# Layer 2: centring of the token norm and the residual sum moved from VectorE to TensorE and ScalarE

## The reference, cut to what matters

```
x   = x + L1(_gn(x))                       # _gn: group norm, 32 groups
tok = [tokens 3136, channels 192]
x1  = _layernorm(tok, g1, b1); x2 = _layernorm(tok, g2, b2)
        # mu = mean over channels; var = mean((x - mu)^2); (x - mu) * rsqrt(var + 1e-5) * g + b
x   = x1 @ W_in_x.T ; z = x2 @ W_in_z.T    # 192 -> 384
y_f = branch(x), y_b = branch(x reversed) reversed
        # branch: conv over 4 tokens, silu, 384 -> 12+16+16, softplus step size,
        # scan h = h * exp(dt * A) + dt * x * B over 3136 tokens and 16 states, y = sum(h * C) + x * D
out = ((y_f + y_b) * silu(z)) @ W_out.T + b_out
```

## Time and profile before

| | |
|---|---|
| median of 3 runs | 20129.69 us |
| profiled execution | 20123.45 us |
| its span, first to last instruction | 20121.7 us |
| mean granted TensorE clock | 0.938 |
| busy: TensorE, VectorE, GpSimd, ScalarE | 87%, 86%, 84%, 70% |
| scans (L1032) | 5376 of 2066 ns |
| outputs (L1240) | 5376 of 1769 ns |

### The profile page before, as it was taken

One profiled execution on the slowest core, in us unless ns is written; L12 is line 12 of the kernel. 1 busy time (PEld: TensorE's weight loads), 2 busy tenths in 40 slices (PEclk: granted clock), 3 DMA queues, 4 the chain that ended last, 5 costly groups with the idle time before them and its releaser, 6 DMA issues. The chain is left out here.

```text
span 20121.7 us, 179901 instructions
## 1 busy us (share of the span) xinstructions
PE 17468.9 (87%) x43392; PEld 7664.0 (38%) x43392; DVE 17219.6 (86%) x13583; ACT 13992.6 (70%) x35077; POOL 16825.7 (84%) x10932
## 2 busy tenths in 40 slices
PE   7888988889888898888988889888898888988889
PEld 3433434334343343433434334343343433434334
DVE  7988979889798897988979789797897978979789
ACT  6767767577676776767767577675776767767677
POOL 6978969789697896978969799696996979969699
PEclk9989989899899998989989899898998989989899
DMA  2313323133231332313323133231332313323233
GB/s 85 135 65 129 137 76 134 65 129 137 76 134 66 128 137 76 134 65 128 137 77 133 66 128 136 77 133 65 129 136 76 134 65 135 130 77 135 73 132 124
DMA packets 528855, 2178.88 MB, mean 108 GB/s; under 512 B 96328, under 2 KB 243424, under 8 KB 527648
## 3 DMA queue, kind: packets, MB, share of 16 engines
q1 hardware_dynamic: 527648, 2165.99, 29.8%
HBM read 1905.47 MB, written 245.63 MB: 107 GB/s over the span
## 5 line engine op out<-in xcount | busy, mean ns | idle before, releaser
L1032 DVE TENSOR_TENSOR_SCAN arena<-ps,arena 128x897 f32<-128x897 f32 x5376 | 10963.7, 2066 | 993.9 <-ACT arena L1188 761.6
L1240 POOL TENSOR_TENSOR arena<-arena 128x896 f32<-128x896 f32 x5376 | 9427.4, 1769 | 901.5 <-PE ps L962 619.8
L962 PE MATMUL ps<-arena,ident 128*128 128x448 f32 x21504 | 8979.4, 556 | 879.6 <-POOL arena L1240 876.2
L1172 ACT ACTIVATE ps<-arena,A 128x448 f32<-128x448 f32 x10752 | 6412.1, 632 | 1749.0 <-DVE arena L1032 1705.3
L962 PEld LDWEIGHTS ps<-arena,ident 128*128 128x128 f32 x21504 | 4049.3, 193 | 5473.3 <-issue 3690.3
L1232 POOL TENSOR_TENSOR arena<-arena 128x896 f32<-128x896 f32 x2688 | 4773.6, 1776 | 0.2 <-DMA arena<-bc_rows 0.2
L1021 DVE TENSOR_TENSOR arena<-ps,arena 128x896 f32<-128x896 f32 x2688 | 2868.0, 1067 | 30.4 <-ACT ps L1134 30.4
L919 PE MATMUL ps<-arena,diag 128*128 128x448 f32 x5376 | 2178.4, 549 | 154.0 <-issue 141.8
L919 PEld LDWEIGHTS ps<-arena,diag 128*128 128x128 f32 x5376 | 1014.8, 192 | 1233.9 <-issue 1097.4
L1094 ACT ACTIVATE arena<-ps,vece 128x448 f32<-128x448 f32 x672 | 423.3, 630 | 948.5 <-PE ps L919 948.5
L1188 ACT ACTIVATE arena<-arena 128x2 f32<-128x2 f32 x5376 | 1045.8, 195 | 50.9 <-DVE arena L1032 50.9
(11 more groups left out here) (160 smaller groups left out, 19406.9 us busy)
## 6 DMA issues: line engine op xcount, KB each, us to landing
arena<-bc_rows SPq DMA_DIRECT2D x1792, 896.0 KB, 5.4
x_projected<-arena SPq DMA_DIRECT2D x112, 672.0 KB, 3.5
y_forward<-arena SPq DMA_DIRECT2D x112, 672.0 KB, 3.9
arena<-x_projected SPq DMA_DIRECT2D x112, 672.0 KB, 7.7
arena<-y_forward SPq DMA_DIRECT2D x112, 672.0 KB, 4.1
x<-in_x SPq DMA_DIRECT2D x119, 336.0 KB, 3.6
x_normed<-arena SPq DMA_DIRECT2D x112, 336.0 KB, 2.8
arena<-x_normed SPq DMA_DIRECT2D x112, 336.0 KB, 4.2
```

The source lines that it names most:

```text
L962: m = e.matmul(y, ident[:, :], pr[:, q % NPR, a * T:a * T + T], start=False, stop=p == NP - 1 and a == 1)
L1032: e.tensor_tensor_scan(rev(hh[:, q % NH, 0:W2], s), rev(decays(q)[:, 0:W2], s), rev(bb[:, q % NB, 0:W2], s), car[:, k, n:n + 1] if i % NC ...
L1172: e.activation(two(decays(q))[:, a, :], dt[:, r % NDT, :], ACT.Exp, scale=Am[s][:, k, 2 * p + a:2 * p + a + 1]).then_inc(c_ex, 1)
L1240: e.tensor_tensor(pr[:, q % NPR, :].rearrange("p (a b) -> p a b", a=2), two(hh[:, q % NH, :]), cr[:, 2 * p:2 * p + 2, :], ALU.mult).then_i ...
```

## The change

The mean and its subtraction become one product with a centring matrix: `cent` holds I - 1/192 (192 x 192). `n1` is now two jobs, one for each half of 96 channels, of 4 matmul instructions each. `nc` is gone. `nq` is two steps on ScalarE at t + 1.5 (it was one at t + 1.9); each squares its half from PSUM into `tmp` and copies the half from PSUM to `nrm`; both wait for the second `n1`. In `o`, each half gets one more matmul (two instructions) that adds `x1` with the identity, and `ou` is a copy with bias on ScalarE, 0.9 slots later, instead of VectorE's sum; the store `out` is 0.9 later. In the forward half `td` has a due time 0.5 later (3.4 for 2.9 after its matmul), and `du` 0.3 later in both. The limit between banks 0 to 3 and WBANK moves from t = 0 to t = -10, so that chunk 1's `n1` (due at -0.2) takes a bank of WBANK. Two memsets of VectorE at the start of the layer's block are moved ahead of the group norm's statistics.

```diff
-        dve.append((t + 2.9, "td", i, e))
-        pool.append((t + 3.9, "du", i, e))
+        dve.append((t + (2.9 if CHUNK[i][0] else 3.4), "td", i, e))
+        pool.append((t + 4.2, "du", i, e))
...
-            dve += [(t + 1.0, "nc", i, 0)]
-            pe += [(t - 0.2, "n1", i, 0), (t + 2.1, "n2", i, 0)]
-            act += [(t + 1.9, "nq", i, 0), (t + 3.0, "nr", i, 0), (t + 4.6, "xh", i, 0)]
+            pe += [(t - 0.2, "n1", i, 0), (t - 0.2, "n1", i, 1), (t + 2.1, "n2", i, 0)]
+            act += [(t + 1.5, "nq", i, 0), (t + 1.5, "nq", i, 1), (t + 3.0, "nr", i, 0), (t + 4.6, "xh", i, 0)]
...
-                dve.append((o + 1.5, "ou", i, k))
-            sp.append((o + 2.5, "out", i, 0))
+                act.append((o + 2.4, "ou", i, k))
+            sp.append((o + 3.4, "out", i, 0))
...
-        banks = WBANK if t >= 0 else [*WBANK, 0, 1, 2, 3]
+        banks = WBANK if t >= -10 else [*WBANK, 0, 1, 2, 3]
...
-                        m = e.matmul(o[0:CP, :], ones[0:CP, 0:CP], nrm[:, i % 2, j * T:j * T + T], start=j == 0, stop=j == 1)
+                        m = e.matmul(o[0:CP, :], cent[:, j, k * CP:(k + 1) * CP], nrm[:, i % 2, j * T:j * T + T],
+                                     start=j == 0, stop=j == 1)
...
-                        m = e.matmul(o[0:CP, :], wout[:, j, k * CP:(k + 1) * CP], gy[:, j, :],
-                                     start=j == 0, stop=j == EJ - 1)
-                    m.then_inc(c_wt, 1)
+                        e.matmul(o[0:CP, :], wout[:, j, k * CP:(k + 1) * CP], gy[:, j, :], start=j == 0, stop=False)
+                    e.matmul(o[0:CP, :], ident[0:CP, 0:CP], x1[:, k, ch(c)], start=False, stop=True).then_inc(c_wt, 1)
...
-                if name == "nc":
-                    filled(w, "n1", i)
-                    b = bank_of("n1", i)
-                    o = nrm[:, i % 2, 0:T]
-                    e.tensor_tensor(o, o, ps[0:CP, b, 0:T], ALU.subtract).then_inc(c_nc, 1)
-                    o = nrm[:, i % 2, T:2 * T]
-                    e.tensor_tensor(o, o, ps[0:CP, b, 0:T], ALU.subtract).then_inc(c_wf[b], 1)
...
-                if name == "ou":
-                    filled(w, "o", i, k)
-                    b = bank_of("o", i, k)
-                    x = x1[:, k, ch(c)]
-                    e.scalar_tensor_tensor(x, ps[0:CP, b, 0:T], bout[:, k:k + 1], x, ALU.add,
-                                           ALU.add).then_inc(c_wf[b], 1)
...
                 if name == "nq":
-                    freed(w, "n1", i)
-                    w.wait_ge(c_nc, i + 1)
+                    filled(w, "n1", i, 1)
                     w.wait_ge(c_nm, 2 * i)
-                    for j in range(CJ):
-                        e.activation(tmp[:, j, :], nrm[:, i % 2, j * T:j * T + T], ACT.Square).then_inc(c_nq, 1)
+                    b = bank_of("n1", i, k)
+                    o = ps[0:CP, b, 0:T]
+                    e.activation(tmp[:, k, :], o, ACT.Square).then_inc(c_nq, 1)
+                    e.activation(nrm[:, i % 2, k * T:k * T + T], o, ACT.Copy).then_inc(c_wf[b], 1)
+                if name == "ou":
+                    filled(w, "o", i, k)
+                    b = bank_of("o", i, k)
+                    e.activation(x1[:, k, ch(c)], ps[0:CP, b, 0:T], ACT.Identity,
+                                 bias=bout[:, k:k + 1]).then_inc(c_wf[b], 1)
```

More of the change, by code:

```diff
@@ L142, in side_schedule @@
         used[b] = used.get(b, 0) + 1
-        if t < 0:
+        if t < -10:
             first = dict(used)
@@ L181, in build @@
     half = sb("half", [128, 1])
+    cent = sb("cent", [CP, CJ, C])
     wx = sb("wx", [CP, CJ, 384])
@@ L218, in build @@
         (ident, d["c_ident"]), (grp, d["c_grp"]), (ones, d["c_ones"]),
+        (cent, d["c_cent"]),
         (w0[:, :, 0:C], d["wk"]), (w0[:, :, C:2 * C], d["wv"]), (w0[:, :, 2 * C:3 * C], d["wr"]),
@@ L827, in build @@
     c_wf = [sem(f"c_free{b}") for b in range(8)]
-    c_ns, c_nc, c_nq, c_nr, c_nm = (sem("c_" + k) for k in ("nsc", "ncen", "nsq", "nrs", "nrm"))
+    c_ns, c_nq, c_nr, c_nm = (sem("c_" + k) for k in ("nsc", "nsq", "nrs", "nrm"))
     c_pad, c_xh, c_c1, c_c2, c_c3, c_c4 = (sem("c_" + k) for k in ("pad", "halo", "crel", "cexp", "cln", "csig"))
@@ L835, in build @@
     s_bl, s_cl = ([sem(f"{k}{G}") for G in range(4)] for k in ("b_loaded", "c_loaded"))
-    sems1 = [n1.v, n1.t, n1.a, c_ex, c_rs, c_bv, c_bp, c_sc, c_ca, c_mc, c_sm, c_ya, c_yv, c_wt, *c_wf, c_ns, c_nc,
+    sems1 = [n1.v, n1.t, n1.a, c_ex, c_rs, c_bv, c_bp, c_sc, c_ca, c_mc, c_sm, c_ya, c_yv, c_wt, *c_wf, c_ns,
              c_nq, c_nr, c_nm, c_pad, c_xh, c_c1, c_c2, c_c3, c_c4, c_t1, c_t2, c_t3, c_du,
@@ L969, in layer1_vector @@
         w = Waits(e)
+        for b in DECAY:
+            e.memset(ps[:, b, T:T1], 0.0)
         w.wait_ge(n1.v, n1.vector(e, w, 0))
         e.memset(xh[0][:, :, 0:3], 0.0).then_inc(c_pad, 1)
-        for b in DECAY:
-            e.memset(ps[:, b, T:T1], 0.0)
         steps = Steps(plan_dve)
@@ L1211, in side @@
                     w.wait_ge(c_nr, i + 1)
-                    freed(w, "n1", i)
+                    freed(w, "n1", i, 1)
                     for j in range(CJ):
@@ L1371 @@
         "c_grp": np.kron(np.eye(CP // 6), np.ones((6, 6)) / 6).astype(np.float32),
+        "c_cent": wt((np.eye(C) - np.full((C, C), 1.0 / C)).astype(np.float32), CP),
         "c_ones": np.full((128, 128), 1.0 / C, np.float32),
```

## The result

The changed kernel takes 20343.74 us (median of 4 runs, 20325.73 to 20372.71) against 20140.47 us (20121.38 to 20151.98); the ratio is 1.0103, 95% interval 1.0086 to 1.0121. The forecast was slower by 101 us to 20231; it is slower by 203. The profiled execution took 20325.73 us.

The account below looks back on a forecast made before the run. Bound: TensorE's dense stretch and GpSimd behind it in backward chunks. 7.5 + 1.4 + 0 - 2.6 + 1.0 - 1.0 = 6.3 us an image, 16 images, +101 us, 20231 us; own range 20185 to 20300, with rivals 20100 to 20345.

Parts of the forecast that it names:

- the backward `du`: Backward half: one `du` moves by a slot on GpSimd, in a dense stretch, at a cost of 0.
- rival (4): Forward chunks: the norm loses its cover, L905 comes 1.5 us later in six chunks, +144 us more, 20375; 8%.
- What bounds: Backward chunks: TensorE's dense stretch, GpSimd's two late outputs and its dense stretch set the time; VectorE's relief gives 0.
- VectorE counts: Backward slots 5 to 9, forward slot 1: outputs wait for scans, so VectorE's relief makes it faster, at most to 19890; 6%.
- The added matmuls, +7.5 us an image: Chunks 8 to 12: the output projection's added matmuls lengthen TensorE's dense stretch by 1.5 us each, +7.5 us an image.
- rival (2): Chunks 8 to 12: the clock takes the cost back if all come to the fast kind, -88 us, 20159; 14%.
- The end of an image, +1.4 forecast: Last projection, behind chunk 13: uncovered matmuls +1.5 us, ScalarE's copy instead of VectorE's sum -0.1, +1.4 in all.
- The clock, -1.0 us an image: Backward half: new chunk lengths shift the clock's falls, -0.2 us a chunk, -1.0 an image.
- `td`, -2.6 us an image: Forward chunks 0 to 5: the first `td` moves behind a scan, so an output loses its 0.43 us wait, -2.6 an image.
- The norm's cover, 0: Forward chunks: the norm's 4 more instructions, 1.5 us, are covered, so L905 stays in place, 0.
- Before the first slot, +1.0: Chain from L893 to L899 before the first slot: between 1 us shorter and +2.5 us by clock, taken as +1.0.

Follow-up runs that it names:

- relief only: Kernel before with `ou` as a copy with bias by ScalarE, without the identity matmuls, residual left out: 20106.09 us, ratio 0.9989.
- the whole edit alone: Kernel before with the output projection's part of the change alone, identity matmuls and ScalarE's copy: 20193.63 us, ratio 1.0038.
- the matmuls alone: Kernel before with the output projection's identity matmuls added and the sum left on VectorE, residual added twice: 20122.70 us, ratio 0.9996.
- the forward part: Kernel before with centring-matrix norm, `td` 0.5 later and `du` 0.35 later in the forward half only: 20086.48 us, ratio 0.9989.
- one edit gave nothing: Kernel before with the change's forward part, plus the second gate matmul `z` due 0.1 earlier: 20127.70 us, ratio 0.9995.
- the other 0.2%: Kernel before with the change's forward part, plus the load of the convolution's input due 4 slots earlier: 20056.74 us, ratio 0.9971.
- both together 0.4%: Kernel before with the change's forward part, plus gate matmul `z` 0.1 earlier and the convolution's input load 4 slots earlier: 20001.46 us, ratio 0.9947.

## Why the prediction was half right

The direction and the bound were right, the size was not: +203 us where +101 was forecast. The step that failed is the backward `du`, put at 0 "in a dense stretch"; it cost 9.6 us an image in the chunks 8 to 12. That the time still lies just inside the range up to 20345 is luck. Its upper end was there for rival (4), a later L905 in forward chunks, which did not come, and layer 1, which the prediction left out, became 5.6 us an image shorter, about 90 us.

- **What bounds.** Right. TensorE's dense stretch and GpSimd's two waits at its end set a backward chunk; VectorE's relief is worth 0 (relief only: +0.1 us a chunk, the rival "VectorE counts" is out). What I missed is that the load of the convolution's input arrives just as TensorE does.
- **The added matmuls, +7.5 us an image.** Right: +6.8 with the whole edit alone, +5.1 with the matmuls alone, less than 7.5 where the low clock at the end became shorter, 1.7 and 1.3 us for 2.6. So rival (2), that the clock takes some of the cost back, holds in part for the matmuls alone. The end of an image, +1.4 forecast: from the start of the last scan to the last instruction 19.1 us became 20.9.
- **`du` in the backward half, "in a dense stretch: 0".** This step failed. I looked at GpSimd, where the move is indeed free: the output of slot 21 comes 0.9 us earlier and that of slot 22 no later. I did not follow the earlier output to TensorE: its idle time before and after the sum of slot 21 becomes one piece of 2.3 us, and the clock falls on the most critical matmuls of the chunk. Undoing this one edit takes 371.6 - 362.0 = 9.6 us from chunks 8 to 12, 9.6 x 16 = 154 us. What is left of their 14.9 us, 5.3, is near the 7.5 - 1.0 = 6.5 forecast.
- **The clock, -1.0 us an image.** Wrong in sign: in chunks 8 to 12 the low clock went from 2.6 to 6.2 us a chunk. With `du` back it is 1.1, so this is the same failed step.
- **`td`, -2.6 us an image.** Half right: -1.9 in chunks 0 to 4, but +1.0 in chunk 5. There t + 4.2 with t = 136.8 in floating point is just below 141, so `du` stays in slot 20 while the `td` that it needs has moved there. GpSimd waits for it in the changed kernel (chunk 5 of image 7), and with 4.25 it doesn't (70.3 us):

```profile
9563.80 1.76 POOL L1234 TENSOR_TENSOR arena<-arena 128x896 f32<-128x896 f32 x1
9567.11 0.98 POOL L1215 TENSOR_TENSOR arena<-arena 128x448 f32<-128x448 f32 x1 [1.54 <-DVE arena L995]
```

- **The norm's cover, 0.** Right. In forward chunk 3 of image 7 the projection waits 0.77 us for GpSimd, as before 0.78; rival (4), that L905 slips, is out. The row shows the first two of the eight instructions, where the view ends:

```profile
9377.73 1.02 PE L907 MATMUL ps<-arena,wx 96*128 96x448 f32 x2 [0.77 <-POOL arena L1209]
```

- **Before the first slot, +1.0.** Half of it: from the first matmul of the norm to GpSimd's multiplication 10.27 us became 10.82, +0.55.
- **The rest.** Between images 5.6 us are left (-3.3 in all, less 1.8 and 0.55). They lie in layer 1, whose code and order are the same; there the time from the last scan to the norm's first matmul runs from 217 to 226 us over the images of the kernel before and from 214 to 218 in the changed kernel. It can hide what a part costs: with the matmuls alone it hid 3.7 us an image. The clock goes with it: between the last scan of an image and the first of the next, TensorE was at the low clock for 107 us on average in the kernel before, for 91 in the changed kernel and with the matmuls alone, and over these stretches in all 13 kernels the length rises by 0.26 us for each us of low clock (correlation 0.85). Two such stretches of the kernel before, behind images 0 and 2, as in the earlier trace rows:

```profile
1270.90:1533.90 263.00, 197.17 (x510) 75.05 (x510) 165.95 (x212) 130.65 (x264) 117.83 (x112) 0.81 0.07 23
3777.90:4049.20 271.30, 205.96 (x513) 77.51 (x511) 167.03 (x212) 130.18 (x263) 116.92 (x112) 0.79 0.07 22
```

  Why unchanged code gets more or less of the low clock stays open. So does chunk 6 (75.4 to 76.8): its low clock is 11.9 us before and 12.3 changed, too little to explain it.

## What to carry to other kernels

An instruction that comes earlier for free can still cost: follow it to the engine that it feeds, and look at the shape of the idle time that it leaves there, one long piece or several short ones, if TensorE's critical matmuls come right behind. Where a schedule is cut into slots by a floor, keep due times off the whole numbers. Before a stretch is shortened at its head, look for every transfer that ends there: here, on top of the forward part, one edit gave nothing, the other 0.2%, and both together 0.4%.

## What the runs showed of the hardware

An idle piece of 2.1 to 2.5 us between two dense bursts brought the granted clock from 2.4 GHz (1.00) to 1.2 GHz (0.50) in 65, 66 and 65 of the 80 chunks of three kernels, 2.8 us of low clock a chunk on average. The same idle time in pieces of up to 0.6 and 1.7 us, with a sum between them, did so in none of the 80 chunks of any of the seven kernels that have it. A wait for a load, at another place and for another instruction, did the same at 2.1 to 2.9 us in 13 of 16 chunks.

The Trainium skill (TensorE: Matmul & The Clock Gate, HAM oscillation) says that idle gaps between bursts bring the low clock back. The traces agree, though the gaps here are shorter than those of the example given there, and show it from both sides: the gap did harm (fall at the head, 2.8 us for 0), and added matmuls went with less low clock at the end of the chunk (1.3 us for 2.6).

The mean over the whole kernel hides all this: the granted clock was 0.938 before and 0.936 after. An image lost 16 us of low clock between the last scan and the next image's first, and gained 18 us in chunks 8 to 12.
